# Second graph layer: neighbours summed on the normalised rows, then projected; logits as VectorE dot products

## The reference, cut to what matters

```python
# layer 0: masked attention
v = relu(x @ Wv + bv); q = relu(x @ Wq + bq); k = relu(x @ Wk + bk)
att = softmax((q @ k.T) * adj - 9e15 * (1 - adj))
x1 = layernorm(x + relu((att @ v) @ Wo + bo))
# layer 1: additive weights over neighbours
h = x1 @ W_w.T + W_b
e, f = h @ a_w[:128], h @ a_w[128:]
u = adj * exp(e[:, None] + f[None, :] + a_b)
out = layernorm(x1 + (u / u.sum(axis=1, keepdims=True)) @ h)
```

## Time and profile before

| | |
|---|---|
| time, 3 runs | 397.88 to 398.65 us, median 398.2 us |
| profiled execution | span of its instructions 397.6 us; 8890 instructions |
| TensorE busy | 382.8 us (96%), 2769 matmuls |
| VectorE, ScalarE, GpSimd busy | 345.1 (87%), 331.2 (83%), 280.4 us (71%) |
| from HBM, to HBM | 75.96 MB, 4.19 MB |

### The profile page before, as it was taken

The page is one execution under the profiler, slowest core; times in us unless marked ns, Lnnn a source line. Parts: engine busy times, 40 slices in busy tenths (PEclk is TensorE's granted clock), DMA queues, the critical chain, the costliest instruction groups (busy, mean ns, idle before and its releaser), DMA issues.

```text
span 397.6 us, 8890 instructions
## 1 busy us (share of the span) xinstructions
PE 382.8 (96%) x2769; PEld 356.5 (90%) x2769; DVE 345.1 (87%) x1056; ACT 331.2 (83%) x661; POOL 280.4 (71%) x258
## 2 busy tenths in 40 slices
PE   8899999999999999999999999999999999999990
PEld 7699988999999999999999998999999999999990
DVE  4887898899779998899969998799988999898976
ACT  5678678997789888898879978898888969999962
POOL 1454862597538995689937999289966799486673
PEclk9999999999999999999999999999999999999997
DMA  7917515836568077663596365870766647968011
GB/s 253 342 43 266 164 65 179 310 122 239 179 219 317 13 281 230 237 249 131 182 298 250 149 235 172 284 296 22 265 202 211 277 157 260 397 220 279 17 55 53
DMA packets 38157, 80.72 MB, mean 203 GB/s; under 512 B 2784, under 2 KB 19680, under 8 KB 38112
## 3 DMA queue, kind: packets, MB, share of 16 engines
q1 hardware_dynamic: 37824, 80.03, 57.7%
q10 hardware_dynamic: 288, 0.14, 0.2%
HBM read 75.96 MB, written 4.19 MB: 202 GB/s over the span
## 4 chain that ended last, share of the span: by engine, by line
PE 87%; DVE 6%; issue 3%; DMA 2%; POOL 1%; SPq 0%; POOLq 0%; DVEq 0%
PE m_ps L1775 14%; PE pt_ps L1727 13%; PE s_ps L1651 7%; PE av_ps L1739 7%; PE av_ps L1741 7%; PE av_ps L1740 7%; PE s_ps L1653 7%; PE s_ps L1652 7%; PE m_ps L1658 6%; PE m_ps L1659 3%; PE m_ps L1651 2%; PE m_ps L1653 2%; PE m_ps L1652 2%; PE m_ps L1756 2%; DMA raw<-in_adj_dram 2%
## 5 line engine op out<-in xcount | busy, mean ns | idle before, releaser
L1041 DVE TENSOR_TENSOR prob_tl<-pt_ps,prob_th 128x512 fp32r<-128x512 f32 x128 | 85.5, 681 | 6.2 <-ACT prob_th L672 6.0
L672 ACT ACTIVATE prob_th<-pt_ps 128x512 fp32r<-128x512 f32 x128 | 74.7, 596 | 18.6 <-PE pt_ps L1727 18.5
L1033 DVE CUSTOM_DVE_ANT_0 prob<-s_ps,penalty 128x1024 f32<-128x1024 f32 x64 | 77.9, 1217 | 10.8 <-PE s_ps L1653 6.6
L404 POOL TENSOR_SCALAR penalty<-raw 128x1024 bf16<-128x1024 f32 x64 | 66.6, 1049 | 26.8 <-DMA raw<-in_adj_dram 13.0
L664 ACT ACTIVATE prob<-prob,neg_max 128x1024 f32<-128x1024 f32 x64 | 73.7, 1152 | 1.9 <-DVE neg_max L1033 1.9
L1727 PE MATMUL pt_ps<-rhs,prob 128*128 128x128 f32 x512 | 73.9, 274 | 0.0
L1739 PE MATMUL av_ps<-prob_th,vh 128*128 128x256 f32 x256 | 73.6, 288 | 0.0
L1741 PE MATMUL av_ps<-prob_th,vl 128*128 128x256 f32 x256 | 72.3, 282 | 0.0
L1740 PE MATMUL av_ps<-prob_tl,vh 128*128 128x256 f32 x256 | 72.3, 282 | 0.0
L606 ACT ACTIVATE adj_t<-adjt_in 128x1024 fp32r<-128x1024 f32 x56 | 59.3, 1062 | 11.2 <-PE m_ps L1775 11.2
L1775 PE MATMUL m_ps<-g,adj_t 128*128 128x258 f32 x448 | 63.1, 287 | 0.4
(11 more groups left out here) (161 smaller groups left out, 918.4 us busy)
## 6 DMA issues: line engine op xcount, KB each, us to landing
raw<-in_adj_dram SPq DMA_DIRECT2D x64, 512.0 KB, 5.6
adjt_in<-in_adj_t_dram SPq DMA_DIRECT2D x56, 512.0 KB, 4.0
x_in<-in_x_dram SPq DMA_DIRECT2D x8, 512.0 KB, 7.0
raw<-in_adj_t_dram SPq DMA_DIRECT2D x8, 512.0 KB, 5.7
raw<-in_x_t_dram SPq DMA_DIRECT2D x15, 256.0 KB, 4.4
out_dram<-out_sb SPq DMA_DIRECT2D x14, 256.0 KB, 4.1
out_dram<-out_sb SPq DMA_DIRECT2D x4, 128.0 KB, 1.8
wb<-in_pack_b_dram SPq DMA_DIRECT2D x1, 320.0 KB, 5.2
```

Source lines behind the costliest of these rows:

```text
L672: sc.activation(prob_th[n % 2][:, tiles(k), (i % 2) * P:(i % 2 + 1) * P], pt_ps[k][:, :].rearrange("p (c n) -> p c n", n=P), ACT.Copy).the ...
L1033: v.tensor_tensor_reduce(out=prob[i % 2][:, :], in0=s_ps[:, :, :].rearrange("p a n -> p (a n)"), in1=penalty[:, n % RING, :], scale=-1.0, ...
L1041: v.tensor_tensor(prob_tl[n % 2][at], pt_ps[k][:, :].rearrange("p (c n) -> p c n", n=P), prob_th[n % 2][at].bitcast(F32), ALU.subtract).th ...
```

## The change

Layer 1 in another order of products. Instead of h = x1 W first, the kernel now forms g = exp(f) x1, sums g over the neighbours, and projects the sum: (sum of exp(f_m) x1_m) W. The bias and the denominator go along: since a row of x1 sums to zero, its last column is redundant; it is replaced by exp(f), and W by W minus its last row, with the bias as last row (raw_wd); two unit columns in w1hl carry the denominator through. e and f come from dot products of the row with two centred vectors (dot_row), on VectorE.

The aggregation has its operands exchanged: g is stationary (high and low part), the adjacency moves, 512 columns, and the result is transposed, as the projection needs it. The host lays adj_t out in other tiles: tile j has, for half j // 4 of the output rows, two chunks of 128 neighbours.

```diff
-            def x1_lo(b, k):
-            def h_out(b, t):
-            def g_lo_den(b):
-            def agg_out(b, i):
+            def dot(b, t):
+                if b == 0 and t == 0:
+                    dve.wait_ge(w1_ok, SET_ALL)
+                wait(dve, ef_done, 2 * (b - 1) + t // TH + 1)
+                dve.wait_ge(x1_done, T * b + t + 1)
+                row_dots(b, t)
+
+            def row_dots(b, t):
+                wait(dve, dots_done, T * b + t - 1)
+                stand_alone(dve)
+                for a in range(2):
+                    last = v.tensor_tensor_reduce(out=spent[:, t % 2, a, :], in0=x1[b % KEPT][:, t, :], in1=dot_row[:, a, :], scale=1.0, scalar=0.0,
+                                                  op0=ALU.mult, op1=ALU.add, accum_out=dots[:, t, a:a + 1])
+                last.then_inc(dots_done, 1)
+
+            def at_lo(b, k):
+                dve.wait_ge(ath_done, 2 * b + k + 1)
+                v.tensor_tensor(half(atl, k), bank["agg", b, k][:, :], half(ath, k).bitcast(F32), ALU.subtract).then_inc(atl_done, 1)
+
+            def hp_out(b, t):
+                if t % TH == 0:
+                    wait(dve, centred, 2 * (b - 1) + t // TH + 1)
+                dve.wait_ge(hp_full, T * b + t + 1)
+                v.tensor_reduce(gs[:, t, :], halves(bank["hp", b, t][:, 0:2 * E1], E1), AX_X, ALU.add).then_inc(hp_done, 1)
...
+            def aggregate(b, j):
+                n = T * b + j
+                k, u = j // TH, j % TH
+                if j == 0:
+                    pe.wait_ge(gl_done, 2 * (b + 1))
+                pe.wait_ge(adjt_done, n + 1)
+                a = shared("agg", b, k) if u == 0 else bank["agg", b, k]
+                for c in range(2):
+                    pe.matmul(a[:, :], g[:, 2 * u + c, 0, :], adj_tile(b, j)[:, c, :], start=(u == 0 and c == 0), stop=False)
+                    last = pe.matmul(a[:, :], g[:, 2 * u + c, 1, :], adj_tile(b, j)[:, c, :], start=False, stop=(u == TH - 1 and c == 1))
+                last.then_inc(agg_full, 1)
+
+            def project_hp(b, t):
+                if b == 0 and t == 0:
+                    pe.wait_ge(w1_ok, SET_ALL)
+                if t % TH == 0:
+                    pe.wait_ge(atl_done, 2 * b + t // TH + 1)
+                hh = shared("hp", b, t)
+                product_side_by_side(hh[:, 0:2 * E1], (blk(ath, t), blk(atl, t)), flat(w1hl[:, :, :]), E1).then_inc(hp_full, 1)
...
+            def aggregate_pair(u):
+                pe.wait_ge(gl_last, u + 1)
+                pe.wait_ge(adjt_last_done, 2 * u + 2)
+                for r in range(TH):
+                    if u == 0:
+                        pe.wait_ge(*((z_done, T * B) if r < 2 else (ptl_done, 2 * T * B + r - 3)))
+                    a = bank["agg", LAST, r][:, 0:PAIR]
+                    for c in range(2):
+                        at = adj_tile(LAST, 2 * u + r // 2)[:, c, (r % 2) * PAIR:(r % 2 + 1) * PAIR]
+                        pe.matmul(a, g[:, 2 * u + c, 0, :], at, start=(u == 0 and c == 0), stop=False)
+                        last = pe.matmul(a, g[:, 2 * u + c, 1, :], at, start=False, stop=(u == TH - 1 and c == 1))
+                    if u == TH - 1:
+                        last.then_inc(sum_last, 1)
```

More of the change, by code:

```diff
@@ new lines, in resnorm_kernel @@
+            ("hp", LAST - 1, 6, 2), ("hp", LAST - 1, 7, 0), ("hp_last", LAST, 0, 2), ("hp_last", LAST, 1, 0), ("hp_last", LAST, 2, 1),
+            ("hp_last", LAST, 3, 0),
+        )
+        bank, before, held = {}, {}, {}
+        for what, b, part, m in (*HEAD_SLOTS, *((what, p - behind, part, m) for p in PASSES
+                                                for what, behind, part, m in PASS_SLOTS if there(p - behind)), *TAIL_SLOTS):
+            bank[what, b, part] = m_ps[m]
+            before[what, b, part] = held.get(m)
+            held[m] = (what, b, part)
@@ L300, in head @@
                 load_x_t(0, 1)
+                load_x_t(1, 0)
                 load_wb()
@@ L747, in g_hi_pair @@
+                for t in range(2 * u, 2 * u + 2):
+                    last = sc.activation(ef[LAST % 2][:, t, :], dots[:, t, :], ACT.Exp, bias=beta[:, :], scale=rstd0[:, t:t + 1])
+                last.then_inc(ef_done, 1)
             def g_hi_pair(u):
@@ L1405, in batch_pass @@
                 if there(p - 2):
-                    agg_out(p - 2, 5)
+                    hp_out(p - 2, 2)
+                prob_lo(p, 2, 1)
+                prob_lo(p, 3, 0)
+                dot(p - 1, 0)
+                dot(p - 1, 1)
+                dot(p - 1, 2)
+                if there(p - 2):
+                    hp_out(p - 2, 3)
+                if there(p - 2):
+                    hp_out(p - 2, 4)
+                prob_lo(p, 3, 1)
+                mask_max(p, 5)
+                dot(p - 1, 3)
@@ L1407, in batch_pass @@
+                dot(p - 1, 4)
+                av_lo(p, 0)
+                dot(p - 1, 5)
+                prob_lo(p, 4, 0)
+                mask_max(p, 6)
+                prob_lo(p, 4, 1)
                 inverse_sum(p, 0)
-                mask_max(p, 4)
+                v_bias(p + 1, 1)
+                v_sum(p + 1, 1)
                 if there(p - 2):
-                    agg_out(p - 2, 6)
+                    hp_out(p - 2, 5)
+                dot(p - 1, 6)
+                dot(p - 1, 7)
+                prob_lo(p, 5, 0)
@@ new lines, in tail @@
+                scale_out(LAST - 2)
+                stats0_pair(1)
+                dot_pair(0)
+                mean_var0_pair(1)
+                prob_lo(LAST, 7, 0)
+                shift0_pair(0)
+                var_eps0_pair(1)
+                prob_lo(LAST, 7, 1)
+                stats1(LAST - 2, 0)
+                o_out_pair(2)
+                mean_var1(LAST - 2, 0)
+                dot_pair(1)
+                residual0_pair(2)
+                stats1(LAST - 2, 1)
+                at_lo(LAST - 1, 0)
@@ new lines, in tail @@
+                mean_var1(LAST - 2, 1)
+                av_lo(LAST, 3)
+                var_eps1(LAST - 2)
+                inverse_sum_pair(3)
+                shift0_pair(1)
+                dot_pair(2)
+                o_out_pair(3)
+                stats0_pair(2)
+                residual0_pair(3)
+                mean_var0_pair(2)
+                stats0_pair(3)
+                hp_out(LAST - 1, 0)
+                var_eps0_pair(2)
+                hp_out(LAST - 1, 1)
+                at_lo(LAST - 1, 1)
```

1366 lines of the change are left out of this document (600 added, 766 removed), and 13 rows, old and new, of tables (HEAD_SLOTS, PASS_SLOTS).

## The result

The changed kernel takes 413.1 us (median of 4, 411.02 to 414.11) against 398.04 (397.69 to 398.65): ratio 1.0364, 95% interval 1.0331 to 1.0398. It is slower by 15 us, where 392.5 was forecast. The profiled execution took 413.68, its span is 411.9, so the sum of 392.0 missed by 19.9. The case that came is rival A, inside its price in the passes (1.9 us a stretch in the mean, 1.5 to 2.5 named), together with an end 8 us longer than forecast.

What follows compares the result with a forecast made beforehand. TensorE's work was taken to bound each pass. 351.3 us before the last transposes, idle 4.3 and end 32.8 gave 388.4; port 2.1 and 1.5 gave 392.0, stated as 392.5 for a run. Range 385 to 405, forecast's own 389 to 396.5.

Steps and rivals of the forecast that it cites:

- rival A: Passes, at dots 0 to 2: VectorE-GpSimd shared port sets the pace; 401 us at 1.5 a stretch, 408 at 2.5; chance 0.24.
- the sum of 392.0: Whole profile: 351.3 us before the last transposes, idle 4.3, end 32.8, port 2.1 and 1.5.
- D: Passes' aggregation: at 0.28 us per 512-column matmul a batch loses 1.3 us; 397 to 399 us; chance 0.14 with Rival B.
- the last sentence of the prediction: Wrong if the pass is not shorter than 46.6 us, or TensorE's work falls by less than 7 us.
- VectorE's price of a dot: Passes, 16 dots each: 0.28 us recorded, about 0.20 occupied, 0.28 with the read; 3.2 to 4.5 us a pass.
- the port waits of the passes: Dots colliding with GpSimd: first six of sixteen a pass; 0.3 us in each of seven stretches, 2.1 us.
- the cheap reading: Passes: VectorE keeps the port once it has it; six dots wait 0.5 us in all, nothing shows.
- Rival A's reasons against: Passes: ten of sixteen dots fall where GpSimd is idle; a delayed pass lets GpSimd get further ahead.
- A's test: Passes: dots' mean over 0.6 us and TensorE idle over 1 us a pass with VectorE named.
- the walk: End, from the last prob transposes: queues followed step by step, 32.8 us, 2.4 longer than before; port adds 1.5.
- Rival B: End: further bank or port waits cost 6 us, 396.5 to 399; a falling clock, 400; chance 0.14 with D.
- The third: the head: Head: first scores can start earlier after reordered loads; idle time from 5.3 to 4.3 us, bounds 3 to 7.

Runs made afterwards that it cites:

- e1: Changed kernel with each dot replaced by a plain sum with one SBUF source (e and f wrong): 398.99 us, 1.0018 to the kernel before.
- e2: Changed kernel without the dots, one copy of two columns per row tile instead (e and f wrong): 399.52 us, 1.0038.
- e13: Reordered e10 (402.1 us) with GpSimd's residual1 and norm1 of batches 5 to 7 on 2 of 128 columns (results wrong): 396.24 us, 0.9951.
- e4: Changed kernel with 18 useless matmuls put into TensorE's waits of the last stretch to hold the clock: 413.99 us, 1.0389.
- e7: e5 with round_last(1) behind ScalarE's last prob_hi in the last stretch: 419.17 us, 1.0537.
- e14: Reordered e10 (402.1 us) with last-batch dots of pairs 0 and 3 moved, projected pair 3 in its own bank: 401.78 us, 1.0075.
- e12: Reordered e10 (402.1 us), half the last adjacency neither loaded nor rounded but for 16 columns a tile (batch 7 wrong): 402.24 us, 1.0107.
- e10: e5 with a product buffer per half batch, VectorE, GpSimd and ScalarE steps reordered, head's loads as in e9: 405.25 us, 1.0174.
- e9: e1 with load_x_t(1,0) back behind load_wb and the first two load_adj, as before the change: 400.02 us, 1.0049.
- e5: Changed kernel with dots of batches 0 to 6 formed by GpSimd multiplying half batches and VectorE reducing: 419.06 us, 1.0497.
- e6: Changed kernel with dots of batches 0 to 6 formed by wide multiplications and reductions, both on VectorE: 423.27 us, 1.0636.

## Why the prediction was wrong, point by point

*TensorE: right.* The aggregation's matmuls step by 0.23 us (timeline of pass 4):

```profile
183.11 0.39 PE L1742 MATMUL m_ps<-adj_t,g 128*128 128x512 f32 x1
183.34 0.39 PE L1743 MATMUL m_ps<-adj_t,g 128*128 128x512 f32 x1
183.57 0.39 PE L1742 MATMUL m_ps<-adj_t,g 128*128 128x512 f32 x1
```

Summed start to start over a pass, aggregation went from 8.02 to 7.67 us (forecast 0.26 off; its own terms, 64 x 0.121 and 32 x 0.232, give 0.32), the 0.79 of transposes are gone, projection is the same. D falls. Without port waits a pass is 45.33 us (e1), below my 45.6 to 46.0. Busy time didn't show it: 383.0, as before, and 376.5 in e1. Records are longer where the granted clock is 0.50 and where a group waits inside, so busy time was a poor test of the work, and the last sentence of the prediction used it.

*VectorE's price of a dot: right* (0.28 recorded, 0.21 from start to start, the read inside it), and worth nothing (e2).

*The step that failed first: the port waits of the passes.* The prediction said "If VectorE keeps the port once it has it, the six wait 0.5 us in all and nothing shows; if GpSimd gets in between each two, they wait 3 to 4 us and 2 to 3 show", and took the first, 0.3 us a stretch. The second is what happens: in pass 4 the blocked dots of 0.79, 1.11, 1.05, 0.69 and 1.34 lose 3.6 us to 0.28, and the pass is 2.4 us over e1's. Where the starts of mask_max(b,0) part between the changed kernel and e1: 1.3 us in the head, 0.1 in pass 1, 11.5 in passes 2 to 6 (1.2, 2.0, 2.4, 1.9 and 3.9), 1.7 in the last; 14.6 us in all by the last prob transposes (369.2 against 354.6). The head's 1.3 are not the port's: no dot has run by the first mask_max, and its first projections step by 0.43 us where e1's step by 0.23. The other 13.2 are the port, where 2.1 had been put. In pass 6 the first six dots met three converts, q_hi and q_lo in one run (301.69 to 306.91), TensorE waited 2.5 us for hp_out and ran 2 us at 0.50 (the second window).

I had ruled for the cheap reading by one row, g_lo_den at 226.04, 0.16 us between two converts. That row lies on the boundary of the two converts, where one instruction gets through; I read it as VectorE keeping the port. One row at a boundary says nothing of the instruction behind it.

The place was off too. I had GpSimd through with the third convert, q_hi and q_lo at 30.5 us of the pass; in pass 4 it is through at 35.7 (215.18, from scores at 179.45). So only two of the six instructions of dots 0 to 2 are held, and three of the four of dots 3 and 4, which I had put where GpSimd idles; the wait that TensorE shows, 1.36 us for av_lo, stands behind these, not at prob_lo(p,3,1) and mask_max(p,5), where the forecast and rival A both looked. Rival A's reasons against were also weaker than I made them: the cover of VectorE was 2 to 3.4 us, the loss 3.6, in the same 10 us as two results that TensorE waits for. The Trainium skill, "SBUF — State Buffer", section "Who interferes with whom", says that issue order decides who blocks. In pass 4 GpSimd's instruction had started before each blocked dot could (convert at 212.05, dot at 212.17), and it was VectorE that waited.

A's test was half wrong too: I asked for a mean of the dots over 0.6, and it was 0.446 with TensorE's idle at 1.67 us. Eleven free dots of sixteen hide five blocked ones in a mean.

*The second: the end.* The forecast counts it from the group behind the last prob transposes, which starts at 369.55: 34.3 us (32.8 and 1.5 for the port), and 42.3 came. Port: up to 6.4 by e13, not 1.5. I had counted g_lo_pair and dot_pair(3) only; shift, a 2-column instruction, waits as long as a wide one (1.16 for 0.15). The other 3.1 us or more are the walk: it had g_lo_pair 0 to 3 at 12.6, 15.5, 17.0 and 18.8, they ended at 16.1, 20.1, 24.5 and 27.0, TensorE at 35.3 instead of 25.3, and part of that remains without GpSimd's wide work: e13's end, counted so, is 35.9 us, 3.1 over the walk's 32.8. Which of its waits carry it isn't settled; e4, e7 and e14 each removed one of 1 to 3 us and another took its place, and e12 took 3.4 us of ScalarE's work off for nothing. Rival B named this, waits for bank and port, at 6 us. It named the clock too: that fell to 0.50 from 386 to 392.2, and in e4, where it didn't fall, the kernel is no faster.

*The third: the head.* Forecast 1.0 us less; batch 1's first mask_max came 2.4 later, 1.1 in e1. Pass 1 made up for it. 1.3 of the 2.4 go with the step of the first projections, which differs between profiles of one head; why it does is open. For the rest the traces have a lead that no run tested: the first projection starts at 5.42 us instead of 4.67, since VectorE now splits x_t (first at 3.88) ahead of the weights.

*The sum.* 392.0 forecast in the profile, 411.9 found: 11.9 us lie ahead of the group behind the last prob transposes (357.7 forecast, 369.55), 8.0 behind its start. In e1, without the dots' port waits, it starts at 355.0, 0.6 us ahead of the sum without its port term (355.6). So of the 11.9, 11.1 are the port term, 13.2 for 2.1; the other 0.7 is the changed kernel's longer head, less what the rest of the sum had too much. The 0.6 us that the prediction adds for a run is too little as well: the profiled execution took 1.8 us more than its span. Against that, e1's profiled run is the fastest of its ten, 1.6 us below their median, so places taken from it are on the early side.

## What to carry to other kernels

Before VectorE gets instructions with two operands in SBUF, count those that fall where GpSimd is busy and reckon with one, at most two, of them getting through per GpSimd instruction, so that every one held costs 0.4 to 1.1 us here, whatever its own size; then ask what stands behind them in VectorE's order. If that sum exceeds the cover of the pass, let GpSimd multiply and VectorE reduce (e10: 45.44 us a pass against 47.69), or give VectorE one SBUF operand. A gain that is shown in a steady pass is still to be paid for at the end: walk it with the port in it, and expect a removed wait of 1 to 3 us to be replaced.

## What the runs showed of the hardware

- A VectorE instruction with two SBUF operands ends with the GpSimd instruction that runs beside it, whatever its size: 128x2, 1.16 us instead of 0.15; 128x128, up to 1.34 instead of 0.28. One or two go through at the boundary of two GpSimd instructions, then the next is held again.
- A cast and a tensor_scalar between SBUF tensors do so too: beside a convert, 1.13 us at 11.03 and 0.86 at 13.35; in e9, with GpSimd idle, 0.28 and 0.27.
- tensor_reduce (275 ns for 128 columns in e1, 1.22 us for 1024 in e5) and mask_max, with one operand in PSUM (1.23 at most), never grew.
- GpSimd lost little against dots (1.40 us for q_lo, 1.29 in e1's mean), 0.35 us where k_lo had started first (a convert of 1.40 at 12.73), and 0.56 us to a wide multiplication (1.60 for 1.04, e6).
- At a granted clock of 0.50 a matmul of 256 columns steps by 0.213 us, at the upper level by 0.117. In the head the step nearly doubles too (512 columns, 0.43 for 0.23) in a stretch whose granted clock reads 1.00.
